# Attention stage: softmax normalised behind the values, with row sums from TensorE and reciprocals from ScalarE

## The reference

```python
x = x + pos + pos_b
y = (x @ color1.T) * alpha1 + beta1               # per pixel, 16 channels
qkv = win @ qkv_w.T + qkv_b                       # win: windows of 64 pixels
attn = softmax(einsum('bhnd,bhmd->bhnm', q * hd ** -0.5, k))
out = einsum('bhnm,bhmd->bhnd', attn, v) @ proj_w.T + proj_b
x = x + out
x = x + gelu(((x @ color2.T) * alpha2 + beta2) @ fc1_w.T + fc1_b) @ fc2_w.T + fc2_b
```

## Time and profile before

| | |
|---|---|
| median of 3 runs | 33319.02 us (33314.83 to 33333.28) |
| the profiled execution | 33304.16 us, its span 33302.7 us |
| busy over the span | PE 91%, DVE 81%, ACT 73%, POOL 35% |
| the attention stage | about the first 7775 us of the span |

### The profile page before, as it was taken

How to read it: one execution, slowest core, us unless ns; L and a number is a source line. 1 busy time by engine, 2 the same in 40 slices (tenths; PEclk the granted TensorE clock), 3 DMA queues, 4 the chain that set the end, 5 groups by cost and what they waited for, 6 DMA issues and landing times. The chain is left out here.

```text
span 33302.7 us, 708247 instructions
## 1 busy us (share of the span) xinstructions
PE 30263.7 (91%) x264406; PEld 14087.6 (42%) x264406; DVE 27134.7 (81%) x28269; ACT 24424.2 (73%) x25873; POOL 11786.8 (35%) x10892
## 2 busy tenths in 40 slices
PE   7888888889998998999899899899989989989999
PEld 5555555554443343343343333343333434433333
DVE  8888888888997998899799799799889979963102
ACT  5666666667997998899799799799889979951010
POOL 2222222223443443444344344344434434431000
PEclk7777777779999999999999999999999999999999
DMA  1111111116998999999899899899999989999757
GB/s 23 20 20 20 19 20 20 20 20 123 175 175 165 175 175 170 169 175 175 165 175 176 165 175 176 165 175 175 174 166 175 175 165 175 175 241 342 234 183 246
DMA packets 2325306, 4877.21 MB, mean 146 GB/s; under 512 B 632480, under 2 KB 764576, under 8 KB 2322464
## 3 DMA queue, kind: packets, MB, share of 16 engines
q0 software_dynamic: 1224320, 3655.97, 61.4%
q1 hardware_dynamic: 945184, 923.44, 10.2%
q10 hardware_dynamic: 154112, 270.62, 2.2%
HBM read 745.98 MB, written 497.03 MB: 37 GB/s over the span
## 5 line engine op out<-in xcount | busy, mean ns | idle before, releaser
L871 PE MATMUL surf_ps<-surf_u,surf_matf 64*64 64x512 f32 x184960 | 20187.8, 594 | 1619.2 <-ACT surf_Cc L918 555.0
L871 PEld LDWEIGHTS surf_ps<-surf_u,surf_matf 64*64 64x64 f32 x184960 | 8267.0, 134 | 13540.9 <-issue 13534.6
L975 POOL DMA_DIRECT2D surf_u<-surf_ds x4080 | 3452.9, 1154 | 3677.5 <-DVE surf_ds L1038 3295.5
L429 POOL TENSOR_TENSOR att_pr<-att_pr,att_rs 128x1024 f32<-128x1024 f32 x1024 | 2083.9, 2055 | 5660.5 <-DVE att_rs L500 5660.5
L1179 PE MATMUL conv_ps<-conv_rows,conv_w 128*96 128x512 f32 x8256 | 3555.1, 593 | 162.9 <-DVE conv_rows L1200 110.9
L1045 DVE SCALAR_TENSOR_TENSOR surf_rH<-surf_Hc,surf_dt_ab,surf_rH 128x1024 f32<-128x1024 f32 x1360 | 1747.1, 1285 | 1955.8 <-ACT surf_rH L901 1556.5
L953 POOL DMA_DIRECT2D surf_Hc<-surf_m x1360 | 1739.2, 1279 | 3668.8 <-DMA surf_Hc<-surf_Ha 3159.3
L968 POOL DMA_DIRECT2D surf_nK<-surf_B x1360 | 1327.5, 976 | 4088.6 <-ACT surf_B L930 3886.9
L926 ACT ACTIVATE surf_p2q<-surf_pq 128x2048 f32<-128x2048 f32 x1360 | 2591.8, 1906 | 133.0 <-DVE surf_pq L1010 126.8
L471 DVE SCALAR_TENSOR_TENSOR att_acc<-att_xin,att_vec,att_acc 128x512 f32<-128x512 f32 x2048 | 2464.2, 1203 | 45.4
L206 PE MATMUL att_t<-att_ident,att_pr 128*128 128x128 f32 x8192 | 1621.7, 331 | 888.7 <-ACT att_pt L329 886.2
(11 more groups left out here) (88 smaller groups left out, 47547.7 us busy)
## 6 DMA issues: line engine op xcount, KB each, us to landing
surf_p2q<-surf_p2q POOLq DMA_DIRECT2D x1360, 512.0 KB, 10.7
surf_Hc<-surf_Ha POOLq DMA_DIRECT2D x1360, 512.0 KB, 12.3
surf_nK<-surf_B POOLq DMA_DIRECT2D x1360, 512.0 KB, 11.7
surf_Hc<-surf_m POOLq DMA_DIRECT2D x1360, 512.0 KB, 9.0
surf_u<-surf_ds POOLq DMA_DIRECT2D x1360, 256.0 KB, 5.4
surf_u<-surf_ds POOLq DMA_DIRECT2D x2720, 128.0 KB, 7.8
conv_rows<-hidden SPq DMA_DIRECT2D x688, 256.0 KB, 4.0
hidden<-conv_outs ACTq DMA_DIRECT2D x688, 192.0 KB, 4.7
```

What stands on the lines that cost most here:

```text
L429: pool.tensor_tensor(pr[:, rg], pr[:, rg], rs[:, rg, :].unsqueeze(2).to_broadcast([P, WC * HEADS, N]), ALU.mult).then_inc(norm_done[rg], 1)
L871: mm = pe.matmul(ps[out, t, :], matf[rows, mat, :], u[rows, k, t, off + 2:off + 2 + W], start=(i == 0), stop=(i == len(taps) - 1))
L975: pool.dma_start(u[rows, k, t, 2:W + 2].rearrange("p a w -> p (a w)"), ds[found, t, :], accum_op=ALU.add).then_inc(u_added, 16)
```

## The change

The exponentials are transposed as they are, and the division comes behind the values. `total`, `norm` and `move_o` go, and GpSimd has no work in this stage. `sums(i)` multiplies the transposed exponentials by a 0/1 matrix `pick` into one bank of `ps_mm`: eight matmuls of 128x32 by 512 columns, which give each output row its denominator. `reciprocals(i)` on ScalarE takes Ln and then Exp of its negative. `divide(i)` on VectorE multiplies the PSUM result of the values by it into `o_sb`. The bias of the values moves into `b_out`, computed once. `pt` grows to two chunks by four groups, and `out_rows` to two pairs, with a semaphore each. The table that is loaded behind the second gelu is `natural_log_exp_and_others`. The lists of all engines are ordered anew, and the loop becomes one of four slots.

```diff
-        pt = sb("pt", [P, 2, WC, P])
+        pt = sb("pt", [P, 2, RG, WC, P])
+        pick = sb("pick", [P, 2, P // RG])
+        rec = sb("rec", [P, T])
-        out_rows = sb("out_rows", [P, WS, 2 * CW])
+        out_rows = sb("out_rows", [P, 2, WS, 2 * CW])
...
-        TURNS = [(1, 0), (0, 0), (0, 1), (1, 1), (3, 0), (2, 1), (2, 0), (3, 1)]
+        TURNS = [(1, 0), (0, 0), (0, 1), (1, 1), (3, 1), (2, 1), (3, 0), (2, 0)]
...
-                pe.wait_ge(norm_done[rg], i + 1)
+                pe.wait_ge(exp_done[rg], i + 1)
...
+            def sums(i, par):
+                pe.wait_ge(t_copied, i * 8 + 8)
+                after(pe, (gelu_done[1], i - 1), (k_split, i + 1))
+                for r in range(2):
+                    for rg in range(RG):
+                        mm = pe.matmul(ps_mm[32 * rg:32 * rg + 32, 0, :], pick[:, r, :], pt[:, par, rg, :, r * N:(r + 1) * N],
+                                       start=(r == 0), stop=(r == 1))
+                mm.then_inc(den_made, 1)
...
-            def slot(i, par):
+            def slot(i, turn4):
+                par = turn4 % 2
                 o = 1 - par
+                value(i - 1, o)
+                turn(i - 1, 2, 1)
+                scores(i, par, 0)
+                fc1(i - 2, par, 0)
+                values(i - 1, o, 0)
+                turn(i - 1, 3, 0)
+                fc1(i - 2, par, 1)
+                turn(i - 1, 2, 0)
+                scores(i, par, 1)
+                sums(i - 1, o)
                 turn(i, 1, 0)
+                values(i - 1, o, 1)
+                turn(i, 0, 0)
                 project(i - 1)
+                turn(i, 0, 1)
                 fc2(i - 2, par)
+                turn(i, 1, 1)
                 query(i + 1, o)
+                turn(i, 3, 1)
                 key(i + 1, o)
...
-            def move_o(i):
...
+            def reciprocals(i):
+                act.wait_ge(den_made, i + 1)
+                wait(act, o_done, i)
+                act.activation(rec[:, :], ps_m[0], ACT.Ln).then_inc(ln_done, 1)
+                act.wait_ge(ln_done, i + 1)
+                act.activation(rec[:, :], rec[:, :], ACT.Exp, scale=-1.0).then_inc(rec_made, 1)
...
+                exps(i - 1, 2)
+                move_t(i - 1, o, 0, 1)
+                move_t(i - 1, o, 1, 1)
+                split_q(i, par)
+                move_t(i - 1, o, 3, 1)
+                split_k(i, par)
+                move_t(i - 1, o, 2, 1)
+                split_v(i - 1, o)
+                gelu(i - 2, par, 0)
+                to_rows(i - 3, (turn4 - 3) % 4)
+                move_t(i - 1, o, 3, 0)
+                gelu(i - 2, par, 1)
+                act.preload_act_table_set("natural_log_exp_and_others")
+                move_t(i - 1, o, 2, 0)
+                exps(i, 1)
                 exps(i, 0)
-                act.preload_act_table_set("exp_and_others")
+                move_t(i, par, 1, 0)
+                reciprocals(i - 1)
+                exps(i, 3)
+                move_t(i, par, 0, 0)
...
-            def total(i, p):
...
+            def divide(i):
+                dve.wait_ge(rec_made, i + 1)
+                dve.wait_ge(pv_made[0], i + 1)
+                dve.wait_ge(pv_made[1], i + 1)
+                wait(dve, proj_made, i)
+                dve.tensor_tensor(o_sb[:, :], ps_o[:, :], rec[:, :], ALU.mult).then_inc(o_done, 1)
...
+                conv(i + 1, o, range(5, 7))
+                top(i, 1)
+                top(i, 0)
+                top(i, 3)
+                top(i, 2)
+                divide(i - 1)
                 conv(i + 1, o, range(7, 8))
                 residual(i - 1, o)
                 conv(i + 1, o, range(8, 10))
                 finish(i - 2, par)
                 conv(i + 2, par, range(0, 5))
```

More of the change, by code:

```diff
@@ L110, in every_slot, with after @@
         def every_slot(eng, slot):
[L112 to L116, removed]
+            for i in range(-2, 9):
+                slot(i, i % 4)
+            with eng.Fori(9, CHUNKS - 3, 4) as i:
+                for k in range(4):
+                    slot(i + k, (1 + k) % 4)
             for i in range(CHUNKS - 3, CHUNKS + 3):
-                slot(i, i % 2)
+                slot(i, i % 4)
         def there(c):
             return not isinstance(c, int) or 0 <= c < CHUNKS
+        def after(eng, *users):
+            for s, c in users:
+                if there(c):
+                    eng.wait_ge(s, c + 1)
+                    return
         block = ctx.enter_context(nc.Block())
@@ L145, in load, with store @@
                     sp.dma_start(xin[w * C:(w + 1) * C, par, :, :], src.rearrange("a c r w -> (a c) r w")).then_inc(x_in[par], 16)
-            def store(k):
+            def store(k, half):
                 b, s, c = place(k, PAIRS)
@@ L178, in _ @@
             pe.wait_ge(w_ready, 1)
+            pe.matmul(ps_mm[:, 0, 4:5], w_proj[:, :], b_qkv[:, 2:3], start=True, stop=True).then_inc(w_made, 1)
+            pe.wait_ge(w_ready, 2)
             def scores(i, par, p):
@@ L229, in fc1 @@
                     pe.wait_ge(x2_done, i + 1)
[L230 to L235, removed]
+                    after(pe, (k_split, i + 2), (y_done, i - 1))
+                    after(pe, (v_split, i + 1))
                 else:
@@ L245, in query @@
                 pe.wait_ge(conv_step, (i + 1) * STEPS_OF_CONV)
-                wait(pe, q_split, i)
-                if there(i - 2):
-                    pe.wait_ge(x2_done, i - 1)
+                after(pe, (x2_done, i - 2), (q_split, i - 1))
                 pe.matmul(ps_m[1], w_qkv[:, 0, :], xs[:, par, :], start=True, stop=True).then_inc(q_made, 1)
@@ L253, in key @@
                     return
-                wait(pe, k_split, i)
-                if there(i - 3):
-                    pe.wait_ge(y_done, i - 2)
+                after(pe, (y_done, i - 3), (rec_made, i - 2), (k_split, i - 1))
                 pe.matmul(ps_m[0], w_qkv[:, 1, :], xs[:, par, :], start=True, stop=True).then_inc(k_made, 1)
@@ L262, in value @@
                     return
[L263 to L266, removed]
+                after(pe, (q_split, i + 1), (x2_done, i - 1))
                 for w in range(WC):
@@ L386, in gelu, with to_rows @@
                                ACT.Gelu, bias=b_fc1[:, 0:1]).then_inc(gelu_done[p], 1)
-            def to_rows(i, par):
+            def to_rows(i, turn4):
                 if not there(i):
                     return
-                if par == 0:
-                    wait(act, out_stored, i * (8 * WR))
+                half, side = turn4 // 2, turn4 % 2
+                if side == 0:
+                    wait(act, out_stored[half], (i - turn4) * (4 * WR))
                 act.wait_ge(y_done, i + 1)
-                act.activation(out_rows[:, :, par * CW:(par + 1) * CW].rearrange("p y (w x) -> p w y x", x=WS),
+                act.activation(out_rows[:, half, :, side * CW:(side + 1) * CW].rearrange("p y (w x) -> p w y x", x=WS),
@@ L573, in attention_weights @@
         ident=np.eye(128, dtype=f),
+        pick=np.stack([(((p[:, None] // 64) == (np.arange(32) // 8) % 2) & (np.arange(32) // 16 == r)).astype(f)
+                       for r in range(2)], axis=1),
         vec=vec)
```

134 lines of the change are left out of this document (41 added, 93 removed).

## The result

The changed kernel takes 32091.29 us (median of 4 runs, 32064.44 to 32113.62), against 33316.93 us before (4 runs, 33308.76 to 33333.28): a ratio of 0.9631, with a 95% interval of 0.9615 to 0.9648. The prediction was 31650, with a range of 31420 to 32500. So the sign and the range hold, but 441 us of the forecast gain are missing, and the time lies just outside the forecast's own band (31420 to 32060). The profiled execution has a span of 32062.8 us.

The account below looks back on a forecast made before the run. Engines waiting in turns, with TensorE's clock falling behind the waits, bounded the attention stage. Slots falling from 30.13 to 23.6 us, times 256, save 1672 us: 33304.16 becomes 31632, plus 15 for the median, 31650; range 31420 to 32500.

Parts of the forecast that it names:

- The store's wait: ScalarE's copy into `out_rows` waits 5.5 us for the previous pair's store in every second slot; forecast to go.
- GpSimd's step: Normalisations ahead of the transposes, 2.06 us each, leave the chain; VectorE's convolution steps beside them gain 3.5 us a slot.
- The loop: Dependences from scores through VectorE, projection and query to the next scores: 23.35 us, taken as 23.6, set the slot.
- hand-over of 0.25: Between `divide` and projection: counted with projection to the residual's start, 1.16, as 1.41 us.
- The further 0.25 for late denominators: Sums, Ln and Exp end just in time or up to 0.5 us late for `divide`; slot taken as 23.6.
- I expect the clock to stay up: TensorE in the attention stage: only short waits of 0.1 to 0.5 us, so granted clock near 1.00.
- the sum (30.13 - 23.6) x 256: Slot time before less slot time forecast, over the attention stage's 256 slots: a gain of 1672 us.
- the part-by-part section: Forecast's pricing per slot: VectorE 18.5 us, ScalarE 18.9, table switch, TensorE 22.1, and the waits.
- Rival 1: TensorE's clock still falls once a slot as some copy is late: slot 28.4 us, time 32880; chance 0.08.
- waits of the new chain: Attention slot of 25.2 to 27 us; chance 0.12, shared with extra table loads or serial column groups in `sums`.
- ratios of 1.70 and 1.85: TensorE's lower against upper clock level, for transposes (1.12 and 0.66 us) and half the scores (3.79 and 2.05).
- queue of 22.1 us: TensorE's work per attention slot at the upper clock level, claimed to lie just under the slot of 23.6 us.

## Why the prediction was right or wrong

*What bound the kernel before.* Right. The store's wait and GpSimd's step are shown by taking each away alone (222 and 725 us). The store's wait was worth less than its own length, as the next late thing took over.

*VectorE.* 3695.62/198 = 18.7 us a slot, forecast 18.5; steps of the convolution 0.750 us, forecast 0.77; `divide` 0.69 for 0.75. *ScalarE.* 18.7 for 18.9; Exp 0.63 as taken, two table loads a slot. *TensorE.* `sums` 379.6/197 = 1.93 us for 2.1; the column groups run side by side. The 2.9 us estimated from the ratio in the Trainium skill (TensorE: Matmul & The Clock Gate, Measured speedup vs the span model) did not come; that ratio is for row tiles, and these are column groups.

*The loop.* Right in kind, 0.4 us too long. Part by part, from the scores' end at 4026.12 + 2.05: to `divide` at 4033.24 it is 5.07 (4.94 forecast); to the projection 0.75; from there to the residual 1.17 (`divide` and these two: 1.92 for 2.16, for the hand-over of 0.25 was counted on top of `divide`); to the query 2.19 (2.20); to the first scores 4.53 (4.53); to the end of the second scores 9.21 (9.52, neighbours that overlap). Sum 22.92, forecast 23.35. The further 0.25 for late denominators never came: `divide` starts 0.34 us behind the end of Exp, as soon as VectorE has finished its tops (the changed kernel's timelines of ScalarE and of VectorE):

```profile
4032.27 0.63 ACT L398 ACTIVATE att_rec<-att_rec 128x512 f32<-128x512 f32 x1
```

```profile
4032.01 1.23 DVE L496 TENSOR_TENSOR att_pr<-att_s,att_mx 128x1024 f32<-128x1024 f32 x1
4033.24 0.69 DVE L506 TENSOR_TENSOR att_o<-att_pv,att_rec 128x512 f32<-128x512 f32 x1
...
4035.16 0.75 DVE L514 SCALAR_TENSOR_TENSOR att_x<-att_m,att_b_out,att_xs 128x512 f32<-128x512 f32 x1 [0.56 <-PE att_m L307]
```

*The step that failed.* "I expect the clock to stay up", and with it the sum (30.13 - 23.6) x 256, in which all slots are alike. The diff said that the loop becomes one of four slots, and the part-by-part section gave that no price, above or below. The missing term is 60 jumps back at some 10 us, 607 us in all. Without it the forecast 31650 would stand against 31484: 0.5% high, from the 0.4 to 0.7 us of the loop. The two misses have opposite signs. The forecast's sum would have needed a rival of this kind: the loop body outgrows what TensorE's sequencer holds. Rival 1 has its second half, a clock that falls, but it falls once every four slots and for another reason.

*The range.* It held, through the case that was set aside for "waits of the new chain" of 25.2 to 27 us. That is a right range for a wrong reason, and so luck: slots without a stall take 22.9 us, and `divide` doesn't wait in them for the new chain.

*Two sums.* By its ratios of 1.70 and 1.85 the queue of 22.1 us takes 37.6 to 40.9 us at the lower level, not 39 to 41; and a slot of 28.9 us gives about 33010, not 32990. Neither moves the forecast.

## What to carry to other kernels

When a change unrolls a loop further, count the instructions of its body on each engine, TensorE first, where one float32 matmul shows as two matmul and two weight-load records, and let each engine loop with its own period: here that added 607 us to the 1226 of the change. Find the loop of dependences that sets the period and prove it by adding one pass inside and one outside. Judge GpSimd not by its busy share, but by which VectorE instructions with two SBUF inputs it meets.

## What the runs showed of the hardware

- A jump back in TensorE's loop cost some 10 us with a body of some 2350 matmul and weight-load records, 4.9 of them standing still; nothing with 1170. The same jump cost 4.8 us elsewhere in the list and 3.9 with 4700 records. In the jump that was looked at, each piece of the stall had one 16 KB packet of the instruction queue in it.
- Behind the stall of 4.9 us in two pieces, the clock was at the lower level (0.50, scores 3.79 us) for some 11 us of work; behind one piece of 3.5 us it was so for some 3 us (projection 1.92 us).
- The convolution's last VectorE step, both inputs in SBUF, took 2.27 us in place of 0.69 beside GpSimd's pair of multiplications; the residual, with one input in PSUM, kept 0.75.
- A VectorE reciprocal took 3.35 us for 128x512 out of PSUM and 0.35 us for 128x32 out of SBUF; Ln and Exp on ScalarE 0.59 and 0.63.
